# State space stage: smallest step folded into the decay's bias and into dt times u, and one row load moved ahead of a store

## The chip, the cores and the metric

The kernel is one program on one core of a Trainium2 chip. The metric is the device time of one execution, in microseconds (us); lower is better. The engines named below are PE (TensorE), DVE (VectorE), ACT (ScalarE), POOL (GpSimd) and SP (SyncE, which here only issues DMAs). They run side by side and meet only at semaphores.

## What is computed

The reference is eight layers on 32 sequences of 256 rows of 128 numbers. The change touches one, a selective state space layer (called L2 attention). On 256 channels with 16 states each it computes:

```python
dt = jax.nn.softplus(dt_low @ W_dt.T + b_dt) + DT_MIN
dt = jnp.clip(dt, DT_MIN, DT_MAX)          # 0.001, 0.1
A = -jnp.exp(log_A)
def step(h, inp):
    dt_t, u_t, B_t, C_t = inp
    dA = jnp.exp(dt_t[:, :, None] * A)
    h = dA * h + (dt_t * u_t)[:, :, None] * B_t[:, None, :]
    y = jnp.einsum('bdn,bn->bd', h, C_t)
    return (h, y)
...
y = (y + u * D_param) * jax.nn.silu(z)
return y @ W_out.T + residual
```

## The kernel before

`state_space` (from line 2104) runs the layer in 16 groups of 512 rows (two sequences). Within a group it goes over the 16 states n = 0 to 15; a tile is 128 partitions by 1024, two halves of 128 channels with 512 rows each. `m = 16 * group + n` counts all steps. For each step:

- ACT writes the decay exp(dt * A_n) into PSUM, two activations of 512 (`decay`, L2376), with A_n as a per-partition scale. It runs two steps ahead of DVE: in iteration n it first does the decay of n + 2, then a piece of `front`.
- SP loads row n of B, spread over the partitions, from a DRAM scratch `brows` (L2181); four buffers, issued three steps ahead.
- POOL multiplies dt*u with that row (`mulB`, L2215), two steps ahead.
- DVE runs the scan over the rows (L2493), and then multiplies with the C row (L2505), which PE has spread into PSUM (L2588). For n = 2 and 5 POOL does this product (L2229).
- PE sums the products over n into two PSUM banks Y (L2621).

While a group is scanned, `front` prepares the next one: ACT, PE and POOL make u, dt, the rows of B and C and the gate. Every engine's instructions are in an order written out by hand: `front` of ACT and PE is cut up by the value of n, and so are `step` of SP and POOL. The steps around the change, all in the group before the one they prepare:

- n = 8, 9: ACT takes the exponential of the raw step (L2338) into `et`. n = 10: POOL caps it (`cap`, L2221), ACT copies the rows of B and C (L2343, L2344).
- n = 11: ACT computes `Ln(et + 1)` (L2347) and then, with an Identity activation, adds `DT_MIN` (held in the tile `least`) and writes `dtA` (L2350). It then copies the first half of the gate out of PSUM (L2355). SP waits for the row copies, stores the rows to `brows` (L2175), and only then issues the load of row n + 3 = 14 of the current group (L2181).
- n = 11, 12: POOL makes the rest of the rows (L2199), the product for row 14, then dt*u of the next group (`steps`, L2234), and overwrites the first column of each sequence in `dtA` with 1e25 (L2236), so that the decay there is zero.
- n = 12, 13: ACT copies the second half of the gate (L2355) and the rest of the rows (L2358), and applies Silu to the gate (L2361); POOL writes the last rows (L2207). n = 13: PE multiplies the group before with W_out (L2608) into the bank M, when the gate has been copied out of it.

`finish` on DVE runs one group late: at its step n = 0 it waits until PE has summed all of Y and multiplies it with the gate (`yy`, L2475). `first()` on ACT and DVE does the preparation of group 0.

ACT has one set of function tables in place at a time: Exp, Ln and Silu each come with an ACT_TABLE_LOAD in the trace where they follow one another.

Of the kernel before, what the change touches and what calls it, by code (L numbers as in the profile page):

```python
# [14 lines left out]
P = 128  # L15
# [2088 lines left out]
def state_space(nc, res, name, load_next):  # L2104
# [3 lines left out]
    with ExitStack() as ctx:  # L2108
# [1 line left out]
        held, loaded, LOADS = res["state"]  # L2110
        win, wk, wdl, wbc, wdt, wout = (held[n] for n in "win cw wdl wbc wdt wout".split())
        cbias, bdt, dpar, lnw, lnb, la, sel = (held[n] for n in "cbias bdt dpar lnw lnb la sel".split())
        A = sc.sb("A", [P, CH, N])
        shift, grow, lower = (sc.sb(n, [P, TILES]) for n in ("shift", "grow", "lower"))
        tmp, dif, var = (sc.sb(n, [P, TILES]) for n in ("tmp", "dif", "var"))
        PADW = S + 3
# [3 lines left out]
        sz = [sc.sb(f"sz{i}", [P, CH, GT]) for i in range(2)]  # L2120
        dtA = [sc.sb(f"dtA{i}", [P, CH, GT]) for i in range(2)]
        dtu = [sc.sb(f"dtu{i}", [P, CH, GT]) for i in range(2)]
        et, least = sc.sb("et", [P, CH, GT]), sc.sb("least", [P, 1])
        dtl, bf, br = sc.sb("dtl", [P, GT]), sc.sb("bf", [P, GT]), sc.sb("br", [P, GT])
        bc = [sc.sb(f"bc{i}", [P, GT], BF16) for i in range(2)]
        Q = 4
# [10 lines left out]
        CC = sc.ps("CC", [P, GT])  # L2137
        M = sc.ps("M", [P, GT])
        brows = nc.dram_tensor(name + "_brows", [2, 2 * N, GT], F32, kind="Internal").ap()
        names = ("set_up seta part var_ready root_ready factored xn_ready f_mm m_read u_ready sz_ready pseq rest_copied bc_ready capped ln_done dt_done dtu_done "  # L2140
                 "dt_ready b_out cc_mm dA_done mulB scanned mulC c_in mulC_pool y_mm y_read out_mm grown summed").split()
        s = {n: sc.sem(n) for n in names}
        block = ctx.enter_context(nc.Block())
# [23 lines left out]
        @block.sync  # L2167
        def _(sp):
            def step(g, k, on):
                if 1 <= g <= 13:  # L2170
                    load_next(sp, g - 1)
                for n in range(N):
                    if on(1) and n == 11:
                        wait(sp, s["m_read"], U * (g + 1) + BF_AT)
                        sp.dma_start(brows[(k + 1) % 2], bf[0:2 * N, :]).then_inc(s["b_out"], 16)  # L2175
                    if on(0) if n < N - 3 else on(1):
                        if n == N - 3:
                            wait(sp, s["b_out"], 16 * (g + 2))
                        kk, nn = (k, n + 3) if n < N - 3 else ((k + 1) % 2, n + 3 - N)
                        wait(sp, s["mulB"], g * N + (n + 3) + 1 - Q)  # L2180
                        sp.dma_start(Bs[nn % Q][:], bass.AP(brows.tensor, (kk * 2 * N + nn) * GT, [[0, P], [1, GT]]))\  # L2181
                            .then_inc(b_in[nn % Q], 16)
                    if on(1) and n == N - 2:
                        wait(sp, s["mulC_pool"], len(MOVED) * (g + 1))
                        for i, nn in enumerate(MOVED):
                            sp.dma_start(Cs[i][:], bass.AP(brows.tensor, ((k + 1) % 2 * 2 * N + N + nn) * GT,
                                                           [[0, P], [1, GT]])).then_inc(s["c_in"], 16)

            straight(sp, step, GROUPS, 1, back=1)

        @block.gpsimd
        def _(pool):
            def rest_of_rows(b, j):

                wait(pool, s["m_read"], U * b + BF_AT)
                wait(pool, s["rest_copied"], b)
                wait(pool, s["mulB"], N * (b - 1) + 14)
                wait(pool, s["capped"], b + 1 if b else 0)
                nc.gpsimd.tensor_tensor(br[64:P], bf[64:P], bc[j][64:P], ALU.subtract).then_inc(s["pseq"], 1)  # L2199
                wait(pool, s["pseq"], b + 1)  # L2200

            def last_rows(b, j):

                wait(pool, s["rest_copied"], b + 1)
                wait(pool, s["mulB"], N * (b - 1) + 16)
                wait(pool, s["dt_ready"], b + 1 if b else 0)
                nc.gpsimd.tensor_tensor(bc[j][96:P], br[96:P], bc[j][96:P], ALU.subtract).then_inc(s["bc_ready"], 1)  # L2207
                wait(pool, s["bc_ready"], b + 1)

            def mulB(m, n, k):  # L2210

                wait(pool, b_in[n % Q], 16 * (m // Q + 1))
                wait(pool, s["dtu_done"], m // N + 1)
                wait(pool, s["scanned"], m + 1 - Q)
                nc.gpsimd.tensor_tensor(inp[n % Q][:], dtu[k][:], Bs[n % Q][:].unsqueeze(1).to_broadcast([P, CH, GT]),  # L2215
                                        ALU.mult).then_inc(s["mulB"], 1)

            def cap(b):

                wait(pool, s["m_read"], U * b + ET_AT)  # L2220
                nc.gpsimd.tensor_scalar(et[:], et[:], CAP, 0.0, ALU.min, ALU.max).then_inc(s["capped"], 1)  # L2221

            def mulC(m, n):

                wait(pool, s["c_in"], 16 * len(MOVED) * (m // N + 1))
                wait(pool, s["scanned"], m + 1)
                wait(pool, s["y_mm"], CH * (m + 1 - Q))
                C = Cs[MOVED.index(n)][:].unsqueeze(1).to_broadcast([P, CH, GT])
                nc.gpsimd.tensor_tensor(hc[n % Q][:], h[n % 2][:], C, ALU.mult).then_inc(s["mulC_pool"], 1)  # L2229

            def steps(b, j):

                wait(pool, s["dt_done"], b + 1)
                nc.gpsimd.tensor_tensor(dtu[j][:], dtA[j][:], u[j][:], ALU.mult).then_inc(s["dtu_done"], 1)  # L2234
                wait(pool, s["dtu_done"], b + 1)
                nc.gpsimd.memset(dtA[j][:].rearrange("p c (b s) -> p (c b) s", b=NB)[:, :, 0:1], 1e25)\  # L2236
                    .then_inc(s["dt_ready"], 1)

            def step(g, k, on):
                for n in range(N):  # L2240
                    if n < N - 2 and on(0):
                        mulB(g * N + (n + 2), n + 2, k)
                    if n - 1 in MOVED and on(0):
                        mulC(g * N + n - 1, n - 1)
                    if on(1) and n == 10 and g >= 0:
                        cap(g + 1)
                    if on(1) and n == 11:
                        rest_of_rows(g + 1, (k + 1) % 2)
                    if on(1) and n == 12 and g >= 0:
                        steps(g + 1, (k + 1) % 2)  # L2250
                    if on(1) and n == 13:
                        last_rows(g + 1, (k + 1) % 2)
                    if n >= N - 2 and on(1):
                        mulB(g * N + (n + 2), n + 2 - N, (k + 1) % 2)

            straight(pool, step, GROUPS, 1, back=1)

        @block.scalar
        def _(act):
# [7 lines left out]
            def first():  # L2267
# [25 lines left out]
                nc.scalar.activation(bf[:], Y[1][:], ACT.Copy)  # L2293
                nc.scalar.activation(bc[0][:], Y[1][:], ACT.Copy).then_inc(s["m_read"], 1)
                wait(act, s["capped"], 1)
                nc.scalar.activation(et[:], et[:], ACT.Ln, bias=1.0).then_inc(s["ln_done"], 1)
                wait(act, s["ln_done"], 1)
                nc.scalar.activation(dtA[0][:], et[:], ACT.Identity, bias=least[:]).then_inc(s["dt_done"], 1)
                wait(act, s["pseq"], 0 + 1)
                nc.scalar.activation(bc[0][64:P], br[64:P], ACT.Copy).then_inc(s["rest_copied"], 1)  # L2300
                for c, bank in ((0, M[:]), (1, dA[1][:, 1])):
# [7 lines left out]
            def front(g, k, n):  # L2309
# [24 lines left out]
                if n in (8, 9):  # L2334
                    c = n - 8
                    wait(act, s["f_mm"], U * b + 5 + c)
                    wait(act, s["dt_done"], b)
                    nc.scalar.activation(et[:, c], M[:], ACT.Exp, bias=bdt[:, c:c + 1]).then_inc(s["m_read"], 1)  # L2338
                if n == 10:
                    wait(act, s["f_mm"], U * b + 7)  # L2340
# [3 lines left out]
                    nc.scalar.activation(bc[j][:], M[:], ACT.Copy).then_inc(s["m_read"], 1)  # L2344
                if n == 11:
                    wait(act, s["capped"], b + 1)
                    nc.scalar.activation(et[:], et[:], ACT.Ln, bias=1.0).then_inc(s["ln_done"], 1)  # L2347
                    wait(act, s["ln_done"], b + 1)
                    wait(act, s["scanned"], N * (b - 1))
                    nc.scalar.activation(dtA[j][:], et[:], ACT.Identity, bias=least[:]).then_inc(s["dt_done"], 1)  # L2350
                if n in (11, 12):
                    c = n - 11
                    wait(act, s["y_read"], CH * g)
# [16 lines left out]
            def decay(m, n, k):  # L2370

                wait(act, s["scanned"], m - 1)
                if m == 1:
                    wait(act, s["m_read"], U)
                for c in range(CH):
                    nc.scalar.activation(dA[m % 2][:, c], dtA[k][:, c], ACT.Exp, scale=A[:, c, n:n + 1])\  # L2376
                        .then_inc(s["dA_done"], 1)

            def step(g, k, on):
# [18 lines left out]
        @block.vector  # L2398
        def _(v):
            stats, mean, rstd, rstd2 = res["stats"], res["mean"], res["rstd"], res["rstd2"]  # L2400
            nc.vector.memset(least[:], DT_MIN)
            nc.vector.memset(xnp[:], 0.0).then_inc(s["set_up"], 1)
            v.wait_ge(loaded, LOADS)
            for c in range(CH):
# [4 lines left out]
            last.then_inc(s["set_up"], 1)  # L2409
            v.wait_ge(s["seta"], 1)  # L2410
            nc.vector.tensor_scalar(A[:], A[:], -1.0, None, ALU.mult).then_inc(s["set_up"], 1)
            done = [0]

            def then(ins):
# [41 lines left out]
            def first():  # L2456
# [2 lines left out]
                nc.vector.tensor_scalar(et[:], et[:], CAP, 0.0, ALU.min, ALU.max).then_inc(s["capped"], 1)  # L2459
                wait(v, s["dt_done"], 1)  # L2460
                wait(v, s["u_ready"], 1)
                nc.vector.tensor_tensor(dtu[0][:], dtA[0][:], u[0][:], ALU.mult).then_inc(s["dtu_done"], 1)
                wait(v, s["dtu_done"], 1)
                nc.vector.memset(dtA[0][:].rearrange("p c (b s) -> p (c b) s", b=NB)[:, :, 0:1], 1e25)\
                    .then_inc(s["dt_ready"], 1)
# [324 lines left out]
```

## Time and profile before

| | us |
|---|---|
| median of 3 runs | 3924.9 (3922.84 to 3928.5) |
| the profiled execution: its own time | 3911.12 |
| the profiled execution: span of the trace | 3908.8 |
| state space stage, first scan to last scan | 2054 to 2973 |

Over the whole span PE is busy 87%, DVE 74%, ACT 49% and POOL 40% of the time. These are averages over eight layers with different limits; only the state space stage, some 920 us, is touched. In a timeline a row gives the start, the duration, the engine, the line, the operation with output and inputs, how many instructions were merged, and in brackets how long the engine sat idle before it and what it then was released by.

### The profile page before, as it was taken

How to read it: one execution, taken by the hardware profiler on the slowest of the kernel's cores; microseconds unless marked ns; L12 is line 12 of the kernel's file. 1: busy time of each engine (PE TensorE's matmuls, PEld its weight loads, DVE VectorE, ACT ScalarE, POOL GpSimd, SP SyncE). 2: the span in 40 equal slices, each digit the busy share in tenths (PEclk: the TensorE clock that was granted, in tenths of full speed). 3: DMA queues.
4: the chain of work that ended last, by engine and by line, in shares of the span. 5: the costliest groups of instructions: out<-in, count | busy, mean ns of one | idle time of the engine just before them, and what ended most of it. 6: DMA issues, size and time to landing. Idle time of an engine off the chain costs nothing. (4 is left out here: it accounts for less than half of the span.)

```text
span 3908.8 us, 60860 instructions
## 1 busy us (share of the span) xinstructions
PE 3396.3 (87%) x21111; PEld 2086.5 (53%) x21164; DVE 2898.4 (74%) x6458; ACT 1905.3 (49%) x3463; POOL 1548.9 (40%) x1015
## 2 busy tenths in 40 slices
PE   5999999887999997587758898888886999999987
PEld 3666676555777763354423343333333666666653
DVE  7888888556777767533229999999997777777765
ACT  2555555324565552222237776777773333333325
POOL 2311111452121210588848888887872011111112
PEclk9999999998999998788879999999998999999989
DMA  6333332004444424233332332222221222222211
GB/s 153 92 88 88 88 89 67 1 2 108 101 101 103 100 62 139 58 43 43 44 73 82 95 105 85 95 85 81 88 87 56 88 88 87 86 88 86 87 58 44
DMA packets 242531, 314.21 MB, mean 80 GB/s; under 512 B 46450, under 2 KB 157779, under 8 KB 231588
## 3 DMA queue, kind: packets, MB, share of 16 engines
q1 hardware_dynamic: 208308, 289.02, 26.4%
q0 software_dynamic: 22528, 17.32, 3.2%
q10 hardware_dynamic: 11392, 3.97, 0.5%
q8 instruction: 173, 2.83, 0.3%
q14 instruction: 130, 1.06, 0.1%
HBM read 251.93 MB, written 57.08 MB: 79 GB/s over the span
## 5 line engine op out<-in xcount | busy, mean ns | idle before, releaser
L574 DVE TENSOR_REDUCE a_Mx<-a_Sx 128x2 f32<-128x512 f32 (+1 forms) x1024 | 590.5, 618 | 173.0 <-PE a_Sx L626 127.2
L2215 POOL TENSOR_TENSOR a_inp<-a_dtu,a_Bs 128x1024 f32<-128x1024 f32 x256 | 597.4, 2360 | 50.0 <-DMA a_Bs<-a_brows 42.5
L2493 DVE TENSOR_TENSOR_SCAN a_h<-a_dA,a_inp 128x1024 f32<-128x1024 f32 x256 | 581.5, 2282 | 21.6 <-ACT a_dA L2376 17.1
L2621 PE MATMUL a_Y<-a_hc,g_ident 128*128 128x512 f32 x1024 | 486.6, 603 | 4.1 <-DVE a_hc L2505 3.4
L347 POOL TENSOR_TENSOR a_rest<-a_qk,a_parts 128x512 f32<-128x512 f32 x64 | 75.1, 1173 | 916.8 <-ACT a_parts L399 916.8
L2376 ACT ACTIVATE a_dA<-a_dtA,a_A 128x512 f32<-128x512 f32 x512 | 330.9, 681 | 141.0 <-DVE a_h L2493 140.1
L413 ACT ACTIVATE a_Pr<-a_SA 128x512 f32<-128x512 f32 x512 | 305.3, 596 | 167.4 <-DVE a_SA L524 79.2
L623 PE MATMUL a_Sx<-att_Kp,att_Qp 96*128 96x256 bf16 (+1 forms) x2048 | 346.1, 261 | 41.2 <-DMA att_Qp<-a_crows 18.3
L1962 ACT ACTIVATE f_sg<-f_GB 128x512 f32<-128x512 f32 x272 | 162.5, 598 | 435.6 <-PE f_GB L2038 435.4
L2088 PEld LDWEIGHTS f_OUT<-g_routed_wd,f_hm 128*128 128x128 f32 x2176 | 280.6, 191 | 124.5 <-issue 90.5
L2621 PEld LDWEIGHTS a_Y<-a_hc,g_ident 128*128 128x128 f32 x1024 | 196.3, 193 | 216.1 <-issue 213.5
L1904 DVE TENSOR_TENSOR f_sg<-f_sg,f_UB 128x512 f32<-128x512 f32 x256 | 175.3, 685 | 167.9 <-PE f_UB L2040 114.0
L2088 PE MATMUL f_OUT<-g_routed_wd,f_hm 128*128 128x128 f32 x2176 | 289.6, 276 | 4.0 <-DVE f_hm L1908 2.4
L2505 DVE TENSOR_TENSOR a_hc<-a_h,a_CC 128x1024 f32<-128x1024 f32 x224 | 273.6, 1221 | 19.0
L416 ACT ACTIVATE a_Pr<-a_SB 128x512 f32<-128x512 f32 (+1 forms) x512 | 253.1, 494 | 60.4 <-PE a_SB L659 36.9
L2038 PE MATMUL f_GB<-f_xnT,g_routed_wg 128*128 128x512 f32 x544 | 280.6, 597 | 0.0
L2040 PE MATMUL f_UB<-f_xnT,g_routed_wu 128*128 128x512 f32 x544 | 277.9, 592 | 0.0
L623 PEld LDWEIGHTS a_Sx<-att_Kp,att_Qp 96*128 96x128 bf16 x2048 | 189.9, 99 | 79.0 <-DVE a_Mx L574 25.7
L1284 POOL DMA_INDIRECT f_sum<-f3e_Y,f3e_idx x128 | 203.4, 1589 | 44.7 <-issue 37.8
L1273 POOL DMA_INDIRECT f3e_xg<-f_rows,f3e_idx x128 | 124.9, 975 | 218.4 <-DVE f3e_idx L1343 179.7
L1908 DVE TENSOR_TENSOR f_hm<-f_sg,f_Cs 128x512 f32<-128x512 f32 x256 | 189.9, 742 | 11.2 <-DMA f_Cs<-f_crows 2.4
L1932 POOL TENSOR_TENSOR f_yroot<-f_yve,f_power 128x4 f32<-128x4 f32 x16 | 16.2, 1010 | 446.0 <-DVE f_yve L1879 446.0
(482 smaller groups left out, 6934.3 us busy)
## 6 DMA issues: line engine op xcount, KB each, us to landing
a_Bs<-a_brows SPq DMA_DIRECT2D x256, 256.0 KB, 3.2
f_Cs<-f_crows SPq DMA_DIRECT2D x512, 128.0 KB, 2.8
att_Qp<-a_packing SPq DMA_DIRECT2D x192, 192.0 KB
att_Kp<-a_packing SPq DMA_DIRECT2D x192, 192.0 KB
a_packing<-a_parts SPq DMA_DIRECT2D x64, 384.0 KB, 2.8
a_packing<-a_parts SPq DMA_DIRECT2D x64, 128.0 KB, 2.8
a_Cs<-a_brows SPq DMA_DIRECT2D x32, 256.0 KB, 4.8
g_x<-x SPq DMA_DIRECT2D x8, 512.0 KB, 7.3
```

Of the source, the lines that this page charges most:

```text
L413: nc.scalar.activation(probs[:, at:at + 2, 0:K0Q], pair(SA[j % 2], K0Q), ACT.Exp)\
L416: nc.scalar.activation(probs[:, at:at + 2, K0Q:K0Q + K1Q], pair(SB, K1Q), ACT.Exp)\
L574: nc.vector.tensor_reduce(Mx[(k + 2 - (j < LATE)) % 2][:, t, 2 * jj:2 * jj + 2], Sx[t][:, 0:2 * wd].rearrange("p (h q) -> p h q", h=2), AX ...
L623: nc.tensor.matmul(both[:, u], Qp[kb][0:KM, h, t * P:t * P + P], Kp[kb][0:KM, h, 0:wd], start=(u == 0), stop=False)
L2038: nc.tensor.matmul(GB[k][:], wg[:, q], xnT[j][:], start=True, stop=True).then_inc(s["g_mm"], 1)
L2040: nc.tensor.matmul(UB[k][:], wu[:, q], xnT[j][:], start=True, stop=True).then_inc(s["u_mm"], 1)
L2088: last = nc.tensor.matmul(OUT[j][:, t], hm[k][:, t * P:t * P + P], wd[:, q], start=False, stop=(q == NQ - 1 and t == G - 1))
L2215: nc.gpsimd.tensor_tensor(inp[n % Q][:], dtu[k][:], Bs[n % Q][:].unsqueeze(1).to_broadcast([P, CH, GT]), ALU.mult).then_inc(s["mulB"], 1)
L2376: nc.scalar.activation(dA[m % 2][:, c], dtA[k][:, c], ACT.Exp, scale=A[:, c, n:n + 1])\
L2493: nc.vector.tensor_tensor_scan(h[n % 2][:].rearrange("p c q -> p (c q)"), dA[m % 2][:].rearrange("p c q -> p (c q)"), inp[n % Q][:].rearra ...
L2505: nc.vector.tensor_tensor(hc[n % Q][:], h[n % 2][:], CC[:].unsqueeze(1).to_broadcast([P, CH, GT]), ALU.mult).then_inc(s["mulC"], 1)
L2621: nc.tensor.matmul(Y[c][:], ident[:], hc[i % Q][:, c], start=(i == 0), stop=(i == N - 1))\
```

## The change

It drops the Identity activation that added `DT_MIN`. `dtA` now holds the softplus alone. The smallest step comes back in two places: the decay's exponential gets a per-partition bias `low = DT_MIN * A_n`, and POOL computes `dtA + DT_MIN` into `et` (now free) before it multiplies with u. For group 0, DVE adds it within the product. DVE makes `low` once at the start. In SP's queue, the store of the rows at n = 11 now comes after the load of row 14, not before it.

```diff
-        A = sc.sb("A", [P, CH, N])
+        A, low = sc.sb("A", [P, CH, N]), sc.sb("low", [P, CH, N])
...
@@ SP, step
                 for n in range(N):
-                    if on(1) and n == 11:
-                        wait(sp, s["m_read"], U * (g + 1) + BF_AT)
-                        sp.dma_start(brows[(k + 1) % 2], bf[0:2 * N, :]).then_inc(s["b_out"], 16)
                     if on(0) if n < N - 3 else on(1):
...
                         sp.dma_start(Bs[nn % Q][:], bass.AP(brows.tensor, (kk * 2 * N + nn) * GT, [[0, P], [1, GT]]))\
                             .then_inc(b_in[nn % Q], 16)
+                    if on(1) and n == 11:
+                        wait(sp, s["m_read"], U * (g + 1) + BF_AT)
+                        sp.dma_start(brows[(k + 1) % 2], bf[0:2 * N, :]).then_inc(s["b_out"], 16)
@@ POOL, steps
                 wait(pool, s["dt_done"], b + 1)
-                nc.gpsimd.tensor_tensor(dtu[j][:], dtA[j][:], u[j][:], ALU.mult).then_inc(s["dtu_done"], 1)
+                nc.gpsimd.tensor_scalar(et[:], dtA[j][:], DT_MIN, 0.0, ALU.add, ALU.max).then_inc(s["raised"], 1)
+                wait(pool, s["raised"], b)
+                nc.gpsimd.tensor_tensor(dtu[j][:], et[:], u[j][:], ALU.mult).then_inc(s["dtu_done"], 1)
@@ ACT, first
-                nc.scalar.activation(et[:], et[:], ACT.Ln, bias=1.0).then_inc(s["ln_done"], 1)
-                wait(act, s["ln_done"], 1)
-                nc.scalar.activation(dtA[0][:], et[:], ACT.Identity, bias=least[:]).then_inc(s["dt_done"], 1)
+                nc.scalar.activation(dtA[0][:], et[:], ACT.Ln, bias=1.0).then_inc(s["dt_done"], 1)
@@ ACT, front, n in (8, 9)
-                    wait(act, s["dt_done"], b)
+                    wait(act, s["dtu_done"], b)
@@ ACT, front, n == 11
-                    nc.scalar.activation(et[:], et[:], ACT.Ln, bias=1.0).then_inc(s["ln_done"], 1)
-                    wait(act, s["ln_done"], b + 1)
                     wait(act, s["scanned"], N * (b - 1))
-                    nc.scalar.activation(dtA[j][:], et[:], ACT.Identity, bias=least[:]).then_inc(s["dt_done"], 1)
+                    nc.scalar.activation(dtA[j][:], et[:], ACT.Ln, bias=1.0).then_inc(s["dt_done"], 1)
@@ ACT, decay
+                if m == 0:
+                    wait(act, s["set_up"], 4)
...
-                    nc.scalar.activation(dA[m % 2][:, c], dtA[k][:, c], ACT.Exp, scale=A[:, c, n:n + 1])\
+                    nc.scalar.activation(dA[m % 2][:, c], dtA[k][:, c], ACT.Exp, scale=A[:, c, n:n + 1],
+                                         bias=low[:, c, n:n + 1])\
@@ DVE, start and first
-            nc.vector.memset(least[:], DT_MIN)
...
+            v.wait_ge(s["set_up"], 3)
+            nc.vector.tensor_scalar(low[:], A[:], DT_MIN, None, ALU.mult).then_inc(s["set_up"], 1)
...
-                nc.vector.tensor_tensor(dtu[0][:], dtA[0][:], u[0][:], ALU.mult).then_inc(s["dtu_done"], 1)
+                nc.vector.scalar_tensor_tensor(out=dtu[0][:], in0=dtA[0][:], scalar=DT_MIN, in1=u[0][:],
+                                               op0=ALU.add, op1=ALU.mult).then_inc(s["dtu_done"], 1)
```

## Rows read from the trace of the kernel before

**Rows 1.** Windows: span, busy us (instructions) of PE, PEld, DVE, ACT, POOL; clock, DMA.

```profile
2200.00:2500.00 300.00, 264.83 (x687) 118.03 (x698) 286.52 (x192) 217.09 (x318) 243.80 (x119) 0.98 0.30 92
```

**Rows 2.** Waits of DVE, 2110 to 2860 us: total us, times, longest us.

```profile
DVE a_h L2493 <- ACT a_dA L2376: 14.8, 26, 0.7
DVE a_yy L2475 <- PE a_Y L2621: 4.7, 13, 1.3
```

**Rows 3.** Timeline of DVE at one border between groups.

```profile
2331.33 1.22 DVE L2505 TENSOR_TENSOR a_hc<-a_h,a_CC 128x1024 f32<-128x1024 f32 x1
2333.23 2.29 DVE L2493 TENSOR_TENSOR_SCAN a_h<-a_dA,a_inp 128x1024 f32<-128x1024 f32 x1 [0.67 <-ACT a_dA L2376]
...
2339.12 1.22 DVE L2505 TENSOR_TENSOR a_hc<-a_h,a_CC 128x1024 f32<-128x1024 f32 x1
2340.81 2.29 DVE L2493 TENSOR_TENSOR_SCAN a_h<-a_dA,a_inp 128x1024 f32<-128x1024 f32 x1 [0.47 <-ACT a_dA L2376]
...
2344.88 1.29 DVE L2475 TENSOR_TENSOR a_yy<-a_Y,a_sz 128x512 f32<-128x512 f32 x2 [0.29 <-PE a_Y L2621]
```

**Rows 4.** Timeline of ACT at the same border.

```profile
2327.81 1.06 ACT L2347 ACTIVATE a_et<-a_et 128x1024 f32<-128x1024 f32 x1
2328.89 1.15 ACT L2350 ACTIVATE a_dtA<-a_et,a_least 128x1024 f32<-128x1024 f32 x1
2329.95 0.58 ACT L2355 ACTIVATE a_sz<-a_M 128x512 f32<-128x512 f32 x1
...
2331.84 1.30 ACT L2376 ACTIVATE a_dA<-a_dtA,a_A 128x512 f32<-128x512 f32 x2
2333.08 0.58 ACT L2355 ACTIVATE a_sz<-a_M 128x512 f32<-128x512 f32 x1
...
2339.31 2.52 ACT L2376 ACTIVATE a_dA<-a_dtA,a_A 128x512 f32<-128x512 f32 x4
```

**Rows 5.** Timeline of PE at the same border; between the two it never idles.

```profile
2333.80 2.02 PE L2608 MATMUL a_M<-g_state_wout,a_yy 128*128 128x128 f32 x16 [0.38 <-ACT a_sz L2355]
...
2341.24 3.60 PE L2621 MATMUL a_Y<-a_hc,g_ident 128*128 128x512 f32 x8
```

**Rows 6.** Instructions of ACT by line and form: busy us, mean ns, idle before.

```profile
L2376 ACT ACTIVATE a_dA<-a_dtA,a_A 128x512 f32<-128x512 f32 x512 | 330.9, 681 | 141.0 <-DVE a_h L2493 140.1
...
L2317 ACT ACTIVATE a_xn<-g_x,a_shift,g_rstd 128x128 f32<-128x128 f32 x60 | 24.5, 478 | 0.0
...
L2321 ACT ACTIVATE a_xnp<-a_M,g_state_lnb,g_state_lnw 128x512 f32<-128x512 f32 x15 | 11.5, 767 | 4.4 <-PE a_M L2556 4.4
...
L1951 ACT ACTIVATE f_e<-f_e 128x128 f32<-128x128 f32 x16 | 5.0, 309 | 1.5 <-DVE f_e L1791 1.4
```

**Rows 7.** Timeline of POOL at the same border.

```profile
2325.38 1.16 POOL L2199 TENSOR_TENSOR a_br<-a_bf,a_bc 64x512 f32<-64x512 f32 x1 [0.82 <-ACT a_bc L2344]
2329.44 2.35 POOL L2215 TENSOR_TENSOR a_inp<-a_dtu,a_Bs 128x1024 f32<-128x1024 f32 x1 [2.90 <-DMA a_Bs<-a_brows]
2331.75 2.36 POOL L2234 TENSOR_TENSOR a_dtu<-a_dtA,a_u 128x1024 f32<-128x1024 f32 x1
```

**Rows 8.** Timeline of SP's queue at the same border.

```profile
2325.33 0.32 SPq L2175 DMA_DIRECT2D a_brows<-a_bf  x1
```

**Rows 9.** The page's DMA issues: count, size, us to landing.

```profile
a_Bs<-a_brows SPq DMA_DIRECT2D x256, 256.0 KB, 3.2
```

**Rows 10.** Instructions of POOL by line: busy us, mean ns, idle before.

```profile
L2221 POOL TENSOR_SCALAR a_et<-a_et 128x1024 f32<-128x1024 f32 x15 | 15.6, 1039 | 71.0 <-ACT a_et L2338 71.0
```

**Rows 11.** Timelines in the next group's middle: ACT's decay of n = 9, DVE's scan of it.

```profile
2370.79 1.30 ACT L2376 ACTIVATE a_dA<-a_dtA,a_A 128x512 f32<-128x512 f32 x2
...
2372.64 2.28 DVE L2493 TENSOR_TENSOR_SCAN a_h<-a_dA,a_inp 128x1024 f32<-128x1024 f32 x1
```

**Rows 12.** Timelines at the start of the stage, POOL and DVE.

```profile
2051.81 13.91 POOL L2215 TENSOR_TENSOR a_inp<-a_dtu,a_Bs 128x1024 f32<-128x1024 f32 x6
...
2054.25 2.29 DVE L2493 TENSOR_TENSOR_SCAN a_h<-a_dA,a_inp 128x1024 f32<-128x1024 f32 x1 [3.40 <-POOL a_inp L2215]
```

More of the change, by code:

```diff
@@ L2122, in state_space @@
         dtu = [sc.sb(f"dtu{i}", [P, CH, GT]) for i in range(2)]
-        et, least = sc.sb("et", [P, CH, GT]), sc.sb("least", [P, 1])
+        et = sc.sb("et", [P, CH, GT])
         dtl, bf, br = sc.sb("dtl", [P, GT]), sc.sb("bf", [P, GT]), sc.sb("br", [P, GT])
@@ L2139, in state_space @@
         brows = nc.dram_tensor(name + "_brows", [2, 2 * N, GT], F32, kind="Internal").ap()
-        names = ("set_up seta part var_ready root_ready factored xn_ready f_mm m_read u_ready sz_ready pseq rest_copied bc_ready capped ln_done dt_done dtu_done "
+        names = ("set_up seta part var_ready root_ready factored xn_ready f_mm m_read u_ready sz_ready pseq rest_copied bc_ready capped raised dt_done dtu_done "
                  "dt_ready b_out cc_mm dA_done mulB scanned mulC c_in mulC_pool y_mm y_read out_mm grown summed").split()
```

## Prediction

> **What bounds the kernel now.** I read the stage before the whole. The windows of the state space stage come first [rows 1]: in 300 us DVE is busy 286.5, PE 264.8, POOL 243.8, ACT 217.1. DVE sets the pace; what an edit is worth is how much of DVE's remaining 4.5% it removes. DVE's waits say where those are [rows 2]: over 13 borders between groups it waits 26 times for a decay, two per border, and once per border for PE's sum. The timeline of one border gives sizes [rows 3]: 0.67 us ahead of the scan of n = 14, 0.47 ahead of the scan of the next group's n = 0, 0.29 ahead of the gated product `yy`; together 1.43 us in each group. The borders repeat, but for the first, where the wait for `yy` is the longest, 1.3. Everywhere else in a group ACT, PE and POOL are ahead of DVE or wait for it.
>
> Then I follow each wait back. Both decays stand behind one unbroken run of ACT [rows 4]: Ln, Identity, gate copy, table load, decay 14, second gate copy, rows copy, decay 15, table load, Silu, table load, decays 0 and 1. Nothing in it waits. The wait for `yy` is the end of an unbroken run of PE [rows 5], from 2333.80 to 2341.24 + 3.60 = 2344.84, and its start was released by ACT's second gate copy (2333.08 + 0.58 = 2333.66). So ACT's run, with the Identity in it, feeds all three waits, though ACT is the least busy of the four.
>
> **The Identity removed.** Before, the gate copy starts 1.08 us after Ln ends (2327.81 + 1.06 = 2328.87 to 2329.95) [rows 4]. Without the Identity it can overlap the end of Ln as it now overlaps the end of the Identity (2328.89 + 1.15 - 2329.95 = 0.09). So 1.17 us leave ACT's run.
>
> **The bias added.** No row shows the decay with a scale and a bias tile, so I bound it. Decay, one operand tile: 681 ns; the 512-wide activation with two such tiles (L2321): 767, 86 more. At 128 wide, none (L1951) 309 and two (L2317) 478: 85 each [rows 6]. At 1024 wide, Identity with one is 1.15 and Ln with none 1.06: 0.09 [rows 4]. The other end is 0: the bias comes free; below that I don't go, because in each of these comparisons the form with more operands is the slower one. I take 0.085, so a decay (two activations) grows by p = 0.17 us. The three comparisons also have other functions or memories, which is why the lower end stays open.
>
> On one border this is paid as follows. Decays 13 and 14 lie ahead of the second gate copy and of scan 14: these gain 1.17 - 2p = 0.83. Decays 13 to 15 and 0 lie ahead of scan 0: its decay gains 1.17 - 4p = 0.49. Then:
> - Scan 14: DVE's wait was 0.67, less than 0.83, so all 0.67 go. It starts at 2332.56, and what comes last is its own product of n = 13 (2331.33 + 1.22) [rows 3].
> - Scan 0: DVE would be ready 0.67 + 0.47 = 1.14 earlier, but the decay comes only 0.49 earlier. The gain shrinks to 0.49 and DVE waits 0.65 here.
> - `yy`: DVE is ready 0.49 + 0.29 = 0.78 earlier, PE's run ends 0.83 earlier. PE's run stays unbroken, as the products of n = 14 and 15 come 0.67 earlier and PE had its work queued up past both (2339.12 + 1.22 = 2340.34 [rows 3], against a use at 2341.24 [rows 5]). The gain is min(0.83, 0.78) = 0.78.
>
> The rest of the group hides the longer decays, as DVE needs each 1.1 us or more after it is ready, but for one. The decay of n = 9 ends at 2370.79 + 1.30 = 2372.09, its scan begins at 2372.64 [rows 11]. Two decays (8 and 9) lie in the run of ACT ahead of it, 0.34; the cover is 0.55, less about 0.09 for the release: 0.12 is left. From p above 0.23 each further 0.1 costs 0.2 here. All in all ACT gets 512 x 0.085 = 43.5 us more and 15 x 1.15 = 17.3 less: it becomes busier, and the kernel gains by where the time lies, not by less work.
>
> The Trainium skill, page "ScalarE: Activation LUTs", section on what ACT_TABLE_LOAD costs, speaks against this edit: each per-partition pointer operand adds about 93 ns to an activation. By this p would be 0.19, the gain of a border 1.46 - 4 x 0.19 = 0.70 instead of 0.78, and the stage's gain 1.2 us smaller; the rows put the price a little lower.
>
> **POOL's new addition, and the load ahead of the store.** These belong together. Before, POOL's product for row 14 waits 2.90 us for its row, to 2329.44 [rows 7], since SP issues that load only behind the store, which itself waited to 2325.33 for ACT's row copies [rows 8]; then 3.2 us of flight [rows 9]. In front of the store the load waits only for a buffer that POOL let go several products earlier, so the row is there before 2325. The product then starts when the rest of rows is done (2325.38 + 1.16 = 2326.54) and ends at 2328.95. Ln, with decay 13 longer, ends at 2329.04. The new tensor_scalar has the form of `cap`, 1.04 us [rows 10]: to 2330.15. dt*u, 2.36, to 2332.6, the memset 0.1, product 15 to 2335.1. Before, dt*u ended at 2331.75 + 2.36 = 2334.11; so POOL is 1.5 us earlier in spite of the addition. Scan 15 begins at 2336.08: cover 0.9 us. The next product, behind the last rows (1.16), is done at 2338.8, scan 0 at 2340.3: 1.5 us. The addition costs nothing. Its bounds: 1.04, or at most 2.36, what a two-tensor product takes; even that makes scan 15 late by only 0.4, which the 0.65 wait ahead of scan 0 absorbs. Behind the new wait `raised` on POOL stand dt*u, the memset and product 15, already counted. On SP nothing is later: the store goes out at the same time, and the loads of rows 15 and 0 move up by one issue. The wait for `dtu_done` at n = 8 was met a group ago.
>
> **The start.** DVE gains a 32-wide operation and loses a memset: about +0.1 us. ACT loses 1.17, and POOL's first product (2051.81) comes forward, until its row lands at about 2050.8 to 2051; scan 0 [rows 12] gains about 0.9. Net 0.8.
>
> **Sum.** There are 15 borders. The first, with a wait of 1.3 at `yy`, goes with PE: 0.83. 14 x 0.78 + 0.83 + 0.8 = 12.5 us. The span goes from 3908.8 to 3896.3, the profiled execution from 3911.1 to 3898.6. The median of the runs lies 13.8 us above the profiled execution; I leave that distance as it is: 3924.9 - 12.5 = 3912.4.
>
> **The rivals.**
> - *The bias is free* (p = 0). For it: no row shows a decay with both; ACT reads two operand tiles at once, perhaps. Against: the three comparisons. Then `yy` gains min(1.17, 1.43) = 1.17: 15 x 1.17 + 0.9 = 18.5, time 3906.4.
> - *The bias is dear.* The decay writes PSUM, none of my comparisons does so with two operands. A border is worth 1.46 - 4p - (2p - 0.46) from p = 0.23 on, which is nothing at p = 0.32. At p = 0.5 it loses 1.08 a group: 16 us slower, 3941. It is slower beyond what can be measured from p = 0.41. Nothing in the trace is near that price.
> - *The row is late after all*: the load ahead of the store waits for something that I don't see. Then POOL's addition has no cover: product 14 ends at 2331.8 as now, product 15 at 2337.7, scan 15 starts at 2337.8 instead of 2336.75, and PE, which waits for its product, ends at 2345.3 instead of 2344.84. That is 0.4 x 15 = 6 us slower, 3931. Decided by whether POOL's row 14 lands after 2328.
> - *Part of the gain goes elsewhere*: the decay of n = 9 is late by a tenth or two, or PE's run has a gap. A gain of 0.3 to 0.5 a border, 5 to 8 us: 3918.
>
> **How the numbers follow.** Forecast 0.62, free bias 0.10, part of the gain lost 0.17, late row 0.05, dear bias 0.06. About 0.2% (8 us) is what a measurement of this kernel can tell from no change. Runs of one kernel lie some 3 us around their median, which I add on both sides. The range goes from the free bias less this, 3904, to the partly lost gain plus this, 3921. Faster by over 0.2%: the forecast, whose 12.5 us are 4.6 above the bound, for the most part, the free bias, and little of the third case: 0.76. Same 0.18, slower 0.06.
>
> **What would show it.** L2376 at about 765 ns, where it was 681. L2350 gone, Ln's line writing `a_dtA`. POOL's product without a wait for `a_Bs`, its tensor_scalar at 1.04 us. In DVE's waits: none ahead of scan 14, 0.65 ahead of scan 0, about nothing ahead of `yy`, and a group shorter by 0.78 us. A new wait at n = 9, or L2376 above 800 ns, would make the sum wrong; so would idle PE between W_out and the last sum of Y.

## The result

The changed kernel is slower, by little more than can be told from no change: 3931.7 us median (18 runs, 3927.6 to 3935.2) against 3924.5 (18 runs, 3918.5 to 3929.3). The ratio is 1.0018, 95% interval 1.0011 to 1.0024, so about 7 us more where 12.5 less were forecast. In the traces the scans of the stage, from the start of the first to that of the last, take 925.4 us instead of 916.9, 0.57 more for each of the 15 borders; its start gained 0.7 us, as forecast. (The profiled execution is 17 us longer than that of before; 8.5 of these arose ahead of the stage, in code that did not change, and the medians do not show them.) The experiments below have their own runs of the kernel before; one of these took 5052.9 us, at a granted clock of 0.65 where the others have 0.96, and no number here uses it.

The page of the changed kernel, costliest groups (busy us, mean ns, idle before and what ended it):

```profile
L2496 DVE TENSOR_TENSOR_SCAN a_h<-a_dA,a_inp 128x1024 f32<-128x1024 f32 x256 | 581.4, 2282 | 33.6 <-POOL a_inp L2215 31.8
L2215 POOL TENSOR_TENSOR a_inp<-a_dtu,a_Bs 128x1024 f32<-128x1024 f32 x256 | 596.4, 2357 | 7.4 <-DVE a_h L2496 3.5
...
L2376 ACT ACTIVATE a_dA<-a_dtA,a_low,a_A 128x512 f32<-128x512 f32 x512 | 377.8, 772 | 142.4 <-DVE a_h L2496 141.4
```

The decay went from 681 [rows 6] to 772 ns, close to what was assumed. What nobody had on the list is in the first line: the scans now wait for POOL. DVE's waits from 2100 to 2900 us, to be set against [rows 2] (this window has 14 borders, that one 13):

```profile
DVE a_h L2496 <- POOL a_inp L2215: 26.4, 28, 1.7
DVE a_yy L2478 <- PE a_Y L2624: 1.5, 1, 1.5
```

All waits for ACT are gone, and 28 waits for POOL stand in their place. One border of DVE, to be set against [rows 3]:

```profile
2348.66 2.29 DVE L2496 TENSOR_TENSOR_SCAN a_h<-a_dA,a_inp 128x1024 f32<-128x1024 f32 x1 [1.71 <-POOL a_inp L2215]
...
2352.44 2.29 DVE L2496 TENSOR_TENSOR_SCAN a_h<-a_dA,a_inp 128x1024 f32<-128x1024 f32 x1 [0.17 <-POOL a_inp L2215]
```

The wait moved by one step: scan 14 no longer waits, scan 15 waits 1.71 us. This border waits 1.88 us in all where it waited 1.43, so the gain on ACT and the loss on POOL nearly cancel. POOL at the same border, to be set against [rows 7]:

```profile
2337.50 2.36 POOL L2215 TENSOR_TENSOR a_inp<-a_dtu,a_Bs 128x1024 f32<-128x1024 f32 x1
2340.01 3.63 POOL L2234 TENSOR_SCALAR a_et<-a_dtA 128x1024 f32<-128x1024 f32 x1 [0.15 <-ACT a_dtA L2348]
2343.73 2.36 POOL L2236 TENSOR_TENSOR a_dtu<-a_et,a_u 128x1024 f32<-128x1024 f32 x1
...
2346.26 2.37 POOL L2215 TENSOR_TENSOR a_inp<-a_dtu,a_Bs 128x1024 f32<-128x1024 f32 x1
```

The wait of 2.90 us for the row is gone, as forecast. But the addition takes 3.63 us, not 1.04. Product 15 ends at 2346.26 + 2.37 = 2348.63, and scan 15 starts at 2348.66.

### The profile page after: what moved, and what is told of

Read it like the earlier page. It is cut to its first block and busy times, and to the rows that moved or that the text cites. A ratio compares the mean times of both kernels' runs of the same rounds, so it can differ in the third digit from the quotient of the medians.

```text
span 3925.9 us, 60860 instructions
## 1 busy us (share of the span) xinstructions
PE 3407.4 (87%) x21111; PEld 2087.5 (53%) x21164; DVE 2899.0 (74%) x6458; ACT 1934.3 (49%) x3447; POOL 1603.0 (41%) x1030
## 3 DMA queue, kind: packets, MB, share of 16 engines
q14 instruction: 130, 1.06, 0.1%
## 5 line engine op out<-in xcount | busy, mean ns | idle before, releaser
L2215 POOL TENSOR_TENSOR a_inp<-a_dtu,a_Bs 128x1024 f32<-128x1024 f32 x256 | 596.4, 2357 | 7.4 <-DVE a_h L2496 3.5
L2376 ACT ACTIVATE a_dA<-a_dtA,a_low,a_A 128x512 f32<-128x512 f32 x512 | 377.8, 772 | 142.4 <-DVE a_h L2496 141.4
L1908 DVE TENSOR_TENSOR f_hm<-f_sg,f_Cs 128x512 f32<-128x512 f32 x256 | 189.9, 742 | 11.3 <-DMA f_Cs<-f_crows 2.5
```

## The experiments

The theory: POOL's addition, at 3.63 us, is the whole cause. Its rivals: the longer decays, the new order of SP's queue, or the mere presence of one more instruction on POOL. All ratios are against runs of the kernel before on the same chip and at the same time. They were taken on two chips, and both give some 3913 us for the kernel before, not 3924.5, so the runs are read by their ratios, or by the difference of medians there. The 95% interval of a ratio reaches some 4 to 5 us to either side. A second measure is the length of the stage in the trace, from one execution each: from the start of the first scan to that of the last it is 916.9 us before and 925.4 after, and it is given for each experiment as "scans".

### POOL's addition at 1.04 us

```diff
-  nc.gpsimd.tensor_scalar(et[:], dtA[j][:], DT_MIN, 0.0, ALU.add, ALU.max).then_inc(s["raised"], 1)
+  nc.gpsimd.tensor_scalar(et[:], dtA[j][:], CAP, 0.0, ALU.min, ALU.max).then_inc(s["raised"], 1)
```

> The changed kernel, with POOL's addition of the smallest step replaced by an instruction of the form of cap (min, then max), so the 0.001 is left out of dt times u for groups 1 to 15. Everything else, the bias on the decay too, stays. Theory (POOL's addition at 3.63 us is what made the kernel slower): it takes 1.04 us, DVE's waits for POOL at the borders go, and the sum of the prediction comes back, 12 us faster than before. Rival (the longer decays with a bias, or the order of SP's queue, made it slower): 7 us slower than before, as the changed kernel.

Measured: 0.9969 (0.9957 to 0.9981), medians 12.5 us faster, scans 905.0. POOL's line and DVE's waits:

```profile
L2234 POOL TENSOR_SCALAR a_et<-a_dtA 128x1024 f32<-128x1024 f32 x15 | 15.6, 1039 | 2.4 <-ACT a_dtA L2348 2.1
```

```profile
DVE a_h L2496 <- ACT a_dA L2376: 11.1, 14, 0.8
DVE a_yy L2478 <- PE a_Y L2624: 1.0, 1, 1.0
```

One wait a border is left, 0.80 us for the decay of the next group's first state (forecast: 0.65), none at scan 14, and only a single one at `yy`. The 0.001 is left out of dt times u here; the version with add and multiply below has it and is as fast, so it is the duration that counts. With this duration changed the prediction's sum holds, and the changed kernel's loss turns into its gain. Bias and queue order are both still in.

### The load ahead of the store, alone

> The kernel before with only the load of row 14 moved ahead of the store. Theory: POOL's wait for its row (2.9 us a group) goes, but DVE waits for ACT there, so the time stays within 1 us of before. Rival (the new order costs, for instance as two transfers collide): slower by some us, with a DVE wait for POOL.

The kernel before, with the store's three lines moved behind the load as in the change. Measured: 1.0004 (0.9995 to 1.0013), scans 916.8. DVE's waits are, to the digit, those of the kernel before in the same window:

```profile
DVE a_h L2493 <- ACT a_dA L2376: 16.0, 28, 0.7
DVE a_yy L2475 <- PE a_Y L2621: 5.0, 14, 1.3
```

The new order costs nothing and by itself gives nothing.

### The changed kernel, store first again

> The changed kernel with SP's queue in the order of before, the store ahead of the load. Theory (POOL's chain at the border, row 14, addition, dt times u, product 15, is what ends last): POOL gets its row 3 us later, product 15 ends some 4 us after DVE wants it, and a border costs about 2.9 us more than before: 40 us slower than before. Rival (POOL's chain is not what ends last): within 3 us of the changed kernel, 7 us slower than before.

Measured: 1.0203 (1.0189 to 1.0217), medians 80 us slower, twice the 40 expected; scans 996.8. POOL's wait for its row is back, scan 15 waits 4.3 us, and `yy` waits for PE besides:

```profile
DVE a_h L2496 <- POOL a_inp L2215: 57.7, 26, 4.5
DVE a_yy L2478 <- PE a_Y L2624: 31.0, 13, 4.3
```

The direction speaks for POOL's chain. The size was missed by 2.4 us a border (80 / 15 = 5.3, against the 2.9 expected), and most of this is PE's clock. PE has no work while DVE waits, then does the last sum of a group. At one border, where scan 15 waited 4.3 us, the timeline and a window (columns as in [rows 1]) show it at half the clock:

```profile
2368.63 0.58 PE L2591 MATMUL a_CC<-a_bc,g_state_sel 128*128 128x512 bf16 x1 [3.75 <-DVE a_hc L2508]
2369.01 6.28 PE L2624 MATMUL a_Y<-a_hc,g_ident 128*128 128x512 f32 x8
```

```profile
2370.00:2374.00 4.00, 4.00 (x6) 1.53 (x5) 2.40 (x6) 3.02 (x6) 4.00 (x3) 0.50 0.37 110
```

The granted clock is 0.50, the 1.2 GHz level, after 3.75 us without a matmul; the same eight matmuls took 3.60 us at full clock [rows 5]. 2.7 us of the 2.89 that `yy` waited at this border are that. It is one of the dearer borders: over all of them the last eight matmuls took 4.9 to 6.3 us, on average 5.7, after 3.5 to 4.3 us without a matmul, and `yy` waited 1.5 to 4.3.

### The bias on the decay, alone

The kernel before with `bias=low[...]` on the decay, `low` all zero.

> The kernel before with a bias tile (all zero) on the decay, and nothing else changed: Identity, POOL and SP as before. Theory (an operand tile costs 0.09 us, 0.18 in a decay): the decays ahead of the scan of n = 14 and of the next group's first scan come 0.36 and 0.72 us later, a border costs 0.35 to 0.45 us more: 5 to 7 us slower than before. Rival (the bias costs nothing where ACT has slack at all other steps): within 2 us.

Measured: 1.0020 (1.0011 to 1.0030), medians 8 us slower, a little more than expected; scans 924.9. The waits for ACT grow from 0.67 and 0.47 to 1.04 and 0.84 us a border, and `yy` waits at only 2 of the 14 borders (0.37 + 0.37 - 0.29 = 0.45 more in all):

```profile
DVE a_h L2498 <- ACT a_dA L2378: 25.6, 28, 1.0
```

So the bias has its price, and the forecast had it right in kind; by chance it is as large as the whole loss of the changed kernel, but the first experiment has it too and is 12.5 us faster.

### The addition at 1.04 us, without the bias

The first experiment with `bias=low[...]` taken off the decay again.

> The changed kernel with POOL's addition at the form of cap and without the bias on the decay: the 0.001 is left out of dt for groups 1 to 15 and of the decay. Theory: ACT's run is 1.17 us shorter and no decay longer: DVE's wait for ACT ahead of the next group's scan (0.80 us with the bias) goes and PE's sum comes last: 17 to 18 us faster than before, 5 more than with the bias. Rival (POOL's chain comes up now): no faster than with the bias, 13 us.

Measured: 0.9959 (0.9945 to 0.9973), medians 17.1 us faster, scans 901.5. DVE waits for ACT at none of the 14 borders from 2100 to 2900 us; what comes last is PE:

```profile
DVE a_yy L2477 <- PE a_Y L2623: 7.2, 14, 1.7
```

### Which tensor_scalar is short on POOL

The kernel before, with ten more instructions on POOL while it sits idle ahead of the stage; input all 0.5, output to another tile but for one, each instruction once. Two such runs, of one execution each.

> The kernel before, with ten more instructions on POOL in its idle time ahead of the state space stage's first work, all over 128x1024 float32, on tiles that are written anew later: the form of cap written to another tile, add then max to another tile and in place, add alone, min alone, max then min, add then multiply, multiply alone, min then add, and a two-tensor add. Theory 1 (the operation decides): every form with add or multiply takes some 3.6 us, min and max alone or together 1.04, wherever they write; two-tensor add 2.36. Theory 2 (writing to another tile than the one read decides): cap's form to another tile takes 3.6, add then max in place 1.04. Theory 3 (the second operand or the pair decides): add alone and min alone are both about 1.04, and add with max 3.6.

> The kernel before, with ten more instructions on POOL in its idle time ahead of the stage, tensor_scalar over 128x1024 float32: add then multiply with 1.0 and with other numbers, multiply then add, subtract then multiply, multiply twice, add twice, multiply then max, add then min, min then max, multiply then subtract. Theory 1 (two pairs are short, add-multiply and min-max in that order): only these take 1.04 us, all others 3.6. Theory 2 (the first operation of the pair being another kind than the second matters, add or multiply with each other short): multiply then add, subtract then multiply and multiply then subtract are 1.04 as well, with max or min 3.6. The numbers used change nothing in either.

Instructions of POOL by line, first run:

```profile
L2199 POOL TENSOR_SCALAR a_inp<-a_inp 128x1024 f32<-128x1024 f32 x1 | 3.8, 3764 | 0.1
L2213 POOL TENSOR_SCALAR a_inp<-a_inp 128x1024 f32<-128x1024 f32 x1 | 3.6, 3637 | 0.1
L2205 POOL TENSOR_SCALAR a_inp<-a_inp 128x1024 f32<-128x1024 f32 x1 | 3.6, 3636 | 0.1
L2211 POOL TENSOR_SCALAR a_inp<-a_inp 128x1024 f32<-128x1024 f32 x1 | 3.6, 3636 | 0.1
...
L2209 POOL TENSOR_SCALAR a_inp<-a_inp 128x1024 f32<-128x1024 f32 x1 | 2.8, 2791 | 0.1
L2201 POOL TENSOR_SCALAR a_inp<-a_inp 128x1024 f32<-128x1024 f32 x1 | 2.8, 2777 | 0.1
L2203 POOL TENSOR_SCALAR a_inp<-a_inp 128x1024 f32<-128x1024 f32 x1 | 2.8, 2775 | 0.1
...
L2197 POOL TENSOR_SCALAR a_inp<-a_inp 128x1024 f32<-128x1024 f32 x1 | 1.1, 1121 | 0.1
...
L2207 POOL TENSOR_SCALAR a_inp<-a_inp 128x1024 f32<-128x1024 f32 x1 | 1.0, 1047 | 0.1
```

L2197 is min then max, L2199 add then max, L2201 add alone, L2203 min alone, L2205 max then min, L2207 add then multiply, L2209 multiply alone, L2211 add then max in place, L2213 min then add. The two-tensor add (L2215) took 2347 ns. Second run, three of ten:

```profile
L2203 POOL TENSOR_SCALAR a_inp<-a_inp 128x1024 f32<-128x1024 f32 x1 | 3.7, 3660 | 0.1
...
L2205 POOL TENSOR_SCALAR a_inp<-a_inp 128x1024 f32<-128x1024 f32 x1 | 1.0, 1047 | 0.1
L2201 POOL TENSOR_SCALAR a_inp<-a_inp 128x1024 f32<-128x1024 f32 x1 | 1.0, 1044 | 0.1
```

There L2201 is multiply then add, L2203 subtract then multiply, L2205 multiply twice. All three theories of the first run fell, and both of the second. Not the operation decides (min alone is long), nor where it writes (in place is as long), nor that there are two (add then max is longer than add alone). It is the ordered pair:

| pair | us |
|---|---|
| min, max; add, multiply (two sets of numbers); multiply, add; multiply, multiply | 1.04 to 1.16 |
| one operation alone: add, min, multiply | 2.78 |
| max, min; min, add; add, max; add, min; add, add; multiply, max; subtract, multiply; multiply, subtract | 3.64 to 3.76 |

Why these four pairs, no run tells.

### The addition as add, then multiply by 1.0

```diff
-  nc.gpsimd.tensor_scalar(et[:], dtA[j][:], DT_MIN, 0.0, ALU.add, ALU.max).then_inc(s["raised"], 1)
+  nc.gpsimd.tensor_scalar(et[:], dtA[j][:], DT_MIN, 1.0, ALU.add, ALU.mult).then_inc(s["raised"], 1)
```

> The changed kernel with POOL's addition written as add 0.001, then multiply by 1.0, in place of add, then max with 0.0: the same result. Theory (the pair of operations sets the duration; add with multiply took 1.05 us on its own, add with max 3.76): 1.04 us in its place too, and the prediction's sum comes back in full, 12 to 13 us faster than before. Rival (the short duration was one of an idle POOL with constant data): 3.6 us and 7 us slower than before, as the changed kernel.

Measured: 0.9968 (0.9956 to 0.9981), medians 13.1 us faster, scans 904.9, and the line takes what the pair took alone:

```profile
L2234 POOL TENSOR_SCALAR a_et<-a_dtA 128x1024 f32<-128x1024 f32 x14 | 14.6, 1044 | 2.2 <-ACT a_dtA L2348 2.0
```

This computes what the changed kernel computes. Two words of the source were the difference between the loss and the gain.

### The addition with two tensors

```diff
+  nc.gpsimd.tensor_tensor(et[:], dtA[j][:], least[:].unsqueeze(2).to_broadcast([P, CH, GT]), ALU.add).then_inc(s["raised"], 1)
```

> The changed kernel with POOL's addition made by a two-tensor add with a broadcast constant tile: the same result. Theory (only the duration of POOL's addition counts): 2.36 us instead of 3.63, product 15 ends at about the time DVE wants it, some 0.4 us late, which DVE's wait ahead of the next scan takes up: 10 to 12 us faster than before. Rival (any further instruction on POOL there is too much): slower than before, or the same.

Measured: 0.9970 (0.9958 to 0.9982), 11.3 us faster, scans 905.8. With the constant broadcast from one column it took 1892 ns:

```profile
L2234 POOL TENSOR_TENSOR a_et<-a_dtA,a_least 128x1024 f32<-128x1024 f32 x15 | 28.4, 1892 | 2.1 <-ACT a_dtA L2348 0.5
```

So an addition of 1.9 us is still covered, and one of 3.6 is not. The 2.36 us that the prediction gave as its upper bound was not reached, so its claim that these would still be free is untried.

### Add, then multiply, with the store first

> As the one with add, then multiply, but with the store ahead of the load in SP's queue, as before the change. Theory (with its row late, POOL's chain has no cover for even 1.04 us; the prediction's rival of the late row): scan 15 about 1 us later than in the kernel before, a border some 0.4 us longer: 4 to 8 us slower than before. Rival (1.04 us fit in without the load ahead): 12 us faster.

Measured: 1.0026 (1.0015 to 1.0037), 9.2 us slower, scans 926.2. POOL waits 41.4 us for rows over 14 borders, and the scans wait for POOL:

```profile
L2215 POOL TENSOR_TENSOR a_inp<-a_dtu,a_Bs 128x1024 f32<-128x1024 f32 x222 | 517.1, 2357 | 43.7 <-DMA a_Bs<-a_brows 41.4
```

```profile
DVE a_h L2496 <- POOL a_inp L2215: 27.9, 28, 2.0
```

This is the prediction's rival of the late row, brought about by the edit: 6 us were forecast for it, 9.2 came. Even the short addition needs the load ahead.

### The smallest step within the logarithm

Ln(c * et + c) with c = exp(0.001) is Ln(et + 1) + 0.001. It needs neither the Identity nor a bias on the decay nor an addition on POOL. On top of the kernel before, with the load ahead:

```diff
-  nc.scalar.activation(et[:], et[:], ACT.Ln, bias=1.0).then_inc(s["ln_done"], 1)
-  wait(act, s["ln_done"], b + 1)
   wait(act, s["scanned"], N * (b - 1))
-  nc.scalar.activation(dtA[j][:], et[:], ACT.Identity, bias=least[:]).then_inc(s["dt_done"], 1)
+  nc.scalar.activation(dtA[j][:], et[:], ACT.Ln, bias=least[:], scale=math.exp(DT_MIN)).then_inc(s["dt_done"], 1)
...
-  nc.vector.memset(least[:], DT_MIN)
+  nc.vector.memset(least[:], math.exp(DT_MIN))
```

> The kernel before with the load ahead of the store, and the smallest step put into the logarithm: Ln(c * et + c) with c = exp(0.001) equals Ln(et + 1) + 0.001, with c as immediate scale and as a bias tile. The Identity goes, and no bias on the decay and no addition on POOL come. Theory (ACT's run of instructions sets the border once POOL's chain is short): 1.17 us less in ACT's run, less 0.09 for the bias tile; a border gains 1.08 to 1.17, in all 17 us faster than before. Rival (something behind ACT's run, PE or DVE, comes up at once): under 8 us faster.

Measured: 0.9960 (0.9947 to 0.9974), medians 15.9 us faster, scans 901.7. The logarithm takes 1.15 us with its bias tile where it took 1.06. It is the fastest of the versions here that compute the layer in full: the intervals of the ratios overlap, but the scans are 3.2 us shorter than with add and multiply. Only the one that leaves out the step and the bias is level with it. What is left at a border is 0.34 us of `yy` for PE (at the first, 1.6):

```profile
DVE a_yy L2471 <- PE a_Y L2617: 6.0, 14, 1.6
```

With the store first, the same version:

> The smallest step within the logarithm, with SP's queue in the order of before. Theory (POOL's chain then ends its product 15 at 2336.65, after the 2336.08 at which DVE would want it, and DVE's slack at the next scan takes that up only in part): 12 to 15 us faster than before, up to 4 less than with the load ahead. Rival (the load ahead is worth nothing here, as POOL has no addition): the same 16 us faster.

Measured: 0.9978 (0.9969 to 0.9987), 8 us faster, scans 910.3: the load ahead is worth 8 us here, twice what was expected at most. The scans wait for POOL, which waits for its row:

```profile
DVE a_h L2489 <- POOL a_inp L2215: 11.7, 27, 0.9
```

## Why the prediction was wrong

**What bounds the kernel.** Right. DVE sets the pace, ACT's run at the border fed the three waits, and shortening that run brought 11.3 to 17.1 us wherever POOL was not late.

**The Identity and the bias.** Right, both somewhat off in size. Without the bias a border gained what the rival of the free bias says: 17.1 and 15.9 us measured for 18.5. The bias took 91 ns a decay instruction where 85 was taken (772 against 681). The wait that stays ahead of the next group's first scan was 0.80 us where 0.65 was forecast. Of these 0.15, the bias is 0.05 (eight instructions). Nearly all of the rest is DVE's step: two scans with no wait between them start 3.51 us apart in the trace of before, which is 0.08 us less than up to the end of the product as its row gives it. So scan 14 comes to 2332.47, not to 2332.56, and DVE stands ready that much earlier. The page "ScalarE: Activation LUTs" of the Trainium skill, section on what ACT_TABLE_LOAD costs, has about 93 ns for each per-partition pointer operand, and this case's trace agrees with it more nearly than with the 85. The decay of n = 9 was not late in the first experiment: no wait there.

**The load ahead of the store.** Right in both halves: worth nothing alone (1.0004), and the cover of what POOL has to do. The experiments with the store first put that cover at 8 us with no addition on POOL, at 22 with the short one (from 13.1 faster to 9.2 slower) and at 72 with the long one (from 7.2 slower to 80 slower), in which PE's clock has its share.

**POOL's addition: the step that failed.** The sum took "The new tensor_scalar has the form of `cap`, 1.04 us", bounded it by "at most 2.36", and concluded "The addition costs nothing". It took 3.63 us. The chain of the prediction is otherwise right to 0.1 us: with 2.59 us more, product 15 ends at 2337.7 on its time scale instead of 2335.1, and scan 15, wanted at 2336.08, is 1.6 late; wanted at 2335.98, by DVE's true step, it is 1.7 late, which is the 1.71 of the trace. The form was the same in shape, type, engine and kind of operands. It differed in writing another tile than it read, which the probe showed to cost next to nothing (1.12 us for min, max), and in the pair of operations: add, max where `cap` has min, max. That second difference was taken for nothing. The upper bound was no bound either: 2.36 us was the row of another kind of instruction, taken over without a row that compares the two kinds. The trace of before had rows that say otherwise, and they should have given the upper end. Beside `cap` POOL has four tensor_scalar instructions in the kernel before, of 1562 to 1609 ns; one of them:

```profile
L321 POOL TENSOR_SCALAR a_below<-att_wd,a_thr 128x512 f32<-128x512 f32 x1 | 1.6, 1567 | 0.0
```

That is a single comparison with a per-partition operand over half as many elements, 1.57 us. Doubled it is an estimate of 3.1, and with 3.1 in the sum scan 15 comes 1.1 us late; the forecast could not have been sure of a gain. A rule of the Trainium skill points the same wrong way: "GPSIMD Engine Reference", section on engine selection, has one-input elementwise work on GpSimd at roughly line rate. The four short pairs agree with that (1.04 us, where DVE's product of the same size takes 1.22 [rows 3]); the other forms do not (2.8 and 3.6 us).

**The rivals.** None named this. The dear operand was thought of on ACT only. The late row was the right mechanism, POOL's chain ending last, with the wrong cause: the row was there in time. That its 3931 is the time measured is luck. The 3.6 us never appeared in the range, so its upper end of 3921 was some 11 us too low.

**What would show it.** The prediction did name the row to look at first ("its tensor_scalar at 1.04 us"), and that row settled the matter.

## What to carry to other kernels

An instruction's price belongs to its exact form, and the operations are part of the form: before a price is taken from a row, compare the operations too, and take the upper end from the slowest row of the same instruction on that engine. On GpSimd, a tensor_scalar over 128x1024 float32 took 1.04 us or 3.6 us depending on the pair of operations, and 2.8 with one alone; where the arithmetic leaves a choice (add with a multiply by 1.0, not with a max by 0.0), it is worth a probe in idle time. When work leaves the engine that ends last, ask which engine is next and how much cover it has left; here the cover was 0.9 us, and the fastest version that computes the layer in full was the one that gave no other engine anything to do.

## What the runs showed of the hardware

- GpSimd's tensor_scalar over 128x1024 float32: 1.04 to 1.16 us for min-max, add-multiply, multiply-add and multiply-multiply; 2.78 us for a single operation; 3.64 to 3.76 for the other pairs tried, the reversed pair max-min among them. With multiply by 1.0 behind it, the addition took 1.04 us instead of 2.78.
- A two-tensor add on GpSimd took 2.35 us with two full tensors and 1.89 with one operand broadcast from a column.
- After a 3.75 us gap PE's next eight matmuls ran at a granted clock of 0.5 and took 6.3 us instead of 3.6, and that version lost 80 us where 40 had been expected without it.
